# Wide attention layers: maxima and scores in two row tiles of 64, token keys in columns of their own, output projection in column tiles

## What is computed

```python
q, k, v = hidden_states @ Wq, encoder_hidden_states @ Wk, encoder_hidden_states @ Wv
logits = einsum('bhqd,bhkd->bhqk', q, k) * 64 ** -0.5
col_bias = zeros((HW, T))
col_bias = col_bias.at[:, token_indices_A].set((-20.0 * (1.0 - mask_A))[:, None])
col_bias = col_bias.at[:, token_indices_B].set((-20.0 * (1.0 - mask_B))[:, None])
probs = softmax(logits + col_bias)
out = einsum('bhqk,bhkd->bhqd', probs, v) @ Wo + bo + hidden_states
```

## Time and profile before

| | us |
|---|---|
| median of three runs | 4634.43 |
| the profiled execution: time | 4641.27 |
| the profiled execution: span, first to last instruction | 4639.5 |
| TensorE busy | 4540.8 (98%) |
| VectorE busy | 2995.0 (65%) |
| GpSimd busy | 2668.0 (58%) |
| ScalarE busy | 2266.8 (49%) |

### The profile page before, as it was taken

The page is one execution under the profiler, slowest core; times in us unless marked ns, Lnnn a source line. Parts: engine busy times, 40 slices in busy tenths (PEclk is TensorE's granted clock), DMA queues, the critical chain, the costliest instruction groups (busy, mean ns, idle before and its releaser), DMA issues.

```text
span 4639.5 us, 56326 instructions
## 1 busy us (share of the span) xinstructions
PE 4540.8 (98%) x20521; PEld 2818.1 (61%) x20521; DVE 2995.0 (65%) x5024; ACT 2266.8 (49%) x4024; POOL 2668.0 (58%) x1278
## 2 busy tenths in 40 slices
PE   8999999999999979999999999999999999999999
PEld 7888765565555445555546655555556655565554
DVE  3321477666766677777846667666757677666765
ACT  3222454454444436666655544444455544454443
POOL 0000377788778601011126887787784877788775
PEclk9999999999999979999999999999999999999999
DMA  4555832222222021111224222221216212222220
GB/s 151 177 186 163 294 74 65 63 68 54 57 63 52 12 49 26 20 26 26 60 88 135 67 52 59 63 68 41 61 45 220 62 36 67 64 68 54 57 47 28
DMA packets 121749, 356.19 MB, mean 77 GB/s; under 512 B 23925, under 2 KB 42357, under 8 KB 109690
## 3 DMA queue, kind: packets, MB, share of 16 engines
q1 hardware_dynamic: 121472, 352.59, 28.3%
HBM read 191.58 MB, written 120.31 MB: 67 GB/s over the span
## 4 chain that ended last, share of the span: by engine, by line
PE 94%; DVE 3%; DMA 1%; issue 1%; SPq 1%; ACT 0%; POOL 0%; DVEq 0%; ACTq 0%
PE ST L946 14%; PE SS L927 13%; PE ST L947 12%; PE OA L957 12%; PE OB L957 11%; PE ST L1079 5%; PE OA L1087 4%; PE SS L992 4%; PE SS L1065 3%; PE OB L1065 1%; PE SS L966 1%; PE ST L1010 1%; PE ST L1011 1%; PE ST L1012 1%; DVE mpart L1588 1%
## 5 line engine op out<-in xcount | busy, mean ns | idle before, releaser
L830 POOL TENSOR_TENSOR acc<-acc,P 128x1024 f32<-128x1024 f32 x912 | 2202.6, 2446 | 597.7 <-DVE acc L1515 584.5
L1266 ACT ACTIVATE P<-ST 128x512 f32<-128x512 f32 (+1 forms) x2496 | 1464.3, 597 | 1304.3 <-PE ST L947 1152.7
L1488 DVE TENSOR_REDUCE mpart<-SS 128x1 f32<-128x400 f32 (+1 forms) x3072 | 1628.5, 570 | 675.8 <-PE SS L927 600.5
L927 PE MATMUL SS<-KS,QS 68*128 68x400 f32 (+1 forms) x3072 | 1038.9, 372 | 11.8 <-DMA QS<-stq 10.2
L946 PE MATMUL ST<-QX,KX 128*128 128x512 f32 (+1 forms) x2496 | 1034.1, 414 | 2.7 <-ACT stw L1173 1.6
L947 PE MATMUL ST<-QS,KS 69*128 69x512 f32 (+1 forms) x2496 | 990.4, 397 | 0.0
L927 PEld LDWEIGHTS SS<-KS,QS 68*128 68x128 f32 x3072 | 584.9, 190 | 221.7 <-DVE mpart L1488 32.1
L946 PEld LDWEIGHTS ST<-QX,KX 128*128 128x128 f32 (+1 forms) x2496 | 464.1, 186 | 387.5 <-issue 286.6
L957 PE MATMUL OA<-P,Vp 128*64 128x512 f32 (+1 forms) x2496 | 658.7, 606 | 0.0
L957 PE MATMUL OB<-P,Vp 128*64 128x512 f32 (+1 forms) x2496 | 641.7, 593 | 0.0
L1348 ACT ACTIVATE PG<-ST 128x512 f32<-128x512 f32 (+1 forms) x832 | 428.0, 616 | 218.5 <-PE ST L1079 218.0
(11 more groups left out here) (238 smaller groups left out, 4240.3 us busy)
## 6 DMA issues: line engine op xcount, KB each, us to landing
q_parts<-stq SPq DMA_DIRECT2D x96, 512.0 KB, 5.1
QX<-q_parts SPq DMA_DIRECT2D x96, 512.0 KB, 11.3
KX<-k_parts SPq DMA_DIRECT2D x48, 801.0 KB, 9.2
QS<-q_parts SPq DMA_DIRECT2D x45, 512.0 KB
R<-R SPq DMA_DIRECT2D x360, 64.0 KB, 2.0
v_tiles<-sv SPq DMA_DIRECT2D x24, 832.0 KB, 6.5
Vp<-v_tiles SPq DMA_DIRECT2D x24, 832.0 KB, 7.3
k_parts<-skh SPq DMA_DIRECT2D x48, 400.5 KB, 4.9
```

Source lines behind the costliest of these rows:

```text
L830: gp.tensor_tensor(out, out, P[0:k, slot(H, t), q, :], ALU.add).then_inc(pool_a, 1)
L927: pe.matmul(SS[at % 3][:, 0:w], QS[H % 3][0:SROWS, qt * 128:(qt + 1) * 128], KS[H % 3][0:SROWS, o:o + w], start=True, stop=True).then_inc( ...
L1266: act.activation(P[0:k, slot(H, t), j, :], ST[n % 3][0:k, :], ACT.Exp, scale=SCALE).then_inc(act_p, 1)
L1488: dve.tensor_reduce(mpart[H % 2][:, i // len(KCH), c:c + 1], SS[RING_AT["s", H, i] % 3][:, 0:w], AX.X, ALU.max).then_inc(dve_ss, 1)
```

## The change

- The head dimension is 64, so the array is used as two row tiles: rows 0 to 63 (tile A) for query parts 0 and 2, rows 64 to 127 (tile B) for parts 1 and 3. Keys stand twice in SBUF (`KH` high parts, `KL` low parts, in both halves), queries are laid out by halves (`QH`, `QL`).
- A unit is now four matmuls of 64 rows (`score`, i = 0 to 3): high by high, high by low, low by high, and a fourth with the bias, mask and maximum rows (`EXK`, `EXQ`). The extra rows no longer fit beside the 64. `step_scores` interleaves the second half of one unit with the first half of the next, which is in the other row tile. The wait for `act_p` and the three banks `ST` stay.
- A maximum tile is one matmul of 64 rows; two, of different halves, go behind each other. Of a step's tiles two go beside the first half of its first unit, two beside the second half of its last, the others in pairs between.
- Token keys: 12 columns (`NTOK`) are appended to the keys, copies of the keys named by the token indices (the context is now fetched by indirect DMA with computed row numbers); their old places are masked with -1e30 in the exponential pass. Only these columns need the bias, so of the maximum tiles only the fourth range adds a small matmul of 12 columns (`EXS`). The last key tile has 78 rows, the fourth range 412 columns. The table of row numbers and the mask are computed by some 30 small VectorE operations ahead of everything else.
- The output projections are two column tiles of 64, all 4 of a step behind `values`; on VectorE their additions stand behind the step's maxima and ahead of `add`.
- Tile 3 of the denominators goes from GpSimd to VectorE, in step 2, ahead of `reciprocals`.
- Row of maxima: 4 DMAs for 1. Keys and queries of a head: 8 DMAs for 7. Two memsets and some loads move.

```diff
+S_FIRST = [14, 14, 12, 12, 12]
+S_NEXT = [10, 10, 10, 10, 10]
+S_THEN = [4, 10]
...
+def s_order():
+
+    out, at = [], [0, 0]
+    for n in S_THEN + S_NEXT:
+        for half in [1, 1] + [0, 1] * ((n - 4) // 2) + [0, 0]:
+            m = at[half]
+            at[half] += 1
+            out.append(((2 * (m // 16) + half) * 4 + m // 4 % 4, m % 4))
+    return out
...
+def s_tiles(h, g):
+
+    if g >= ROW_STEP:
+        first = sum(S_THEN[:g - ROW_STEP])
+        return 2, (range(first, first + S_THEN[g - ROW_STEP]) if h + 2 < HEADS else range(0))
+    counts = S_FIRST if h == 0 else S_NEXT
+    first = (0 if h == 0 else sum(S_THEN)) + sum(counts[:g])
+    return 1, (range(first, first + counts[g]) if h + 1 < HEADS else range(0))
...
+def o_items(h, g):
+
+    return range(4 * g, 4 * g + 4) if h % 2 == 1 and h >= 3 and g < 2 else range(0)
...
-    return [1, 2] if h + 1 < HEADS else [1, 2] + list(range(5, KT - 2))
+    return [1, 2, 3] if h + 1 < HEADS else [1, 2, 3] + list(range(6, KT - 2))
...
-    return list(range(3, KT if h + 1 < HEADS else 5))
+    return list(range(4, KT if h + 1 < HEADS else 6))
...
             def load_head_k(H):
-                b, n = H % 3, H // 2
-                sp.dma_start(words(KS[b][0:D, :]), dK[n, H % 2, 0, :, :]).then_inc(d_s[b], 16)
-                sp.dma_start(words(KS[b][D:D + NROWS, :]), dExt[H // HEADS, :, :]).then_inc(d_s[b], 16)
-
-            def load_head_b(H):
-                sp.dma_start(words(QS[H % 3][D:SROWS, :]), dBias.rearrange("m r q -> (m r) q")).then_inc(d_s[H % 3], 16)
+                for r in range(0, 128, 64):
+                    sp.dma_start(words(KH[H % 3][r:r + D, :]), dK[H // 2, H % 2, 0, :, :]).then_inc(d_s[H % 3], 16)
 
             def load_head_kx(H):
-                sp.dma_start(words(KX[H % 2][:, :]), dK[H // 2, H % 2, :, :, :].rearrange("r d k -> (r d) k"))\
-                    .then_inc(d_x[H % 2], 16)
+                for r in range(0, 128, 64):
+                    sp.dma_start(words(KL[H % 2][r:r + D, :]), dK[H // 2, H % 2, 1, :, :]).then_inc(d_x[H % 2], 16)
...
             def max_row(H):
                 sp.wait_ge(dve_ss, DVE_AT["m", H, 0])
-                sp.dma_start(words(QS[H % 3][MXROW:MXROW + 1, :]).rearrange("o (t p) -> o t p", p=128),
-                             words(mrow[:, :])).then_inc(d_m, 16)
+                for j in range(JQ):
+                    r, q = 64 * (j % 2) + MXROW, slice(j // 2 * 512, j // 2 * 512 + 512)
+                    sp.dma_start(words(EXQ[H % 2][r:r + 1, q]).rearrange("o (t p) -> o t p", p=128),
+                                 words(mrow[4 * j:4 * j + 4, :])).then_inc(d_m, 16)
...
+            gp.wait_ge(dve_tab, 22)
+            for t in range(KT):
+                gp.indirect_dma_start(c_land[0:rows_of(t), t, :], None, a["ctx"][:, :],
+                                      bass.IndirectOffsetOnAxis(ap=t_row[0:rows_of(t), t:t + 1], axis=0))\
+                    .then_inc(d_cin[t], 16)
...
             def s_tile(H, i):
-                at = RING_AT["s", H, i]
+                at, (qt, c) = RING_AT["s", H, i], s_place(H % HEADS, i)
                 if i == 0:
                     pe.wait_ge(d_s[H % 3], s_loaded(H))
+                    pe.wait_ge(d_ex, 64 * (H // HEADS + 1))
+                    pe.wait_ge(d_eq, 96)
                 wait_ring(pe, at)
-                qt, (o, w) = i // len(KCH), KCH[i % len(KCH)]
-                pe.matmul(SS[at % 3][:, 0:w], QS[H % 3][0:SROWS, qt * 128:(qt + 1) * 128], KS[H % 3][0:SROWS, o:o + w],
-                          start=True, stop=True).then_inc(pe_s, 1)
+                r, q = slice(qt // 4 % 2 * 64, qt // 4 % 2 * 64 + 64), qt // 8 * 512 + qt % 4 * 128
+                o, w = KCH[c]
+                last = pe.matmul(SS[at % 3][:, 0:w], QH[H % 3][r, q:q + 128], KH[H % 3][r, o:o + w],
+                                 start=True, stop=o + w < KP)
+                if o + w == KP:
+                    last = pe.matmul(SS[at % 3][:, w - NTOK:w], EXQ[H % 2][r, q:q + 128], EXS[r, :], start=False, stop=True)
+                last.then_inc(pe_s, 1)
...
-            def scores(H, t, j):
+            def score(H, t, j, i):
+
                 n, k = HU * H + JQ * t + j, rows_of(t)
-                if t == 0 and j == 0:
-                    pe.wait_ge(d_x[H % 2], 48 * (H // 2 + 1))
-                    pe.wait_ge(d_m, 16 * (H + 1))
-                u = n % (HU * HEADS)
-                if u < 3:
-                    pe.wait_ge(act_qw, QITEMS * (H // HEADS) + max(i for i in range(QITEMS) if i % 3 == n % 3) + 1)
-                wait(pe, act_p, n - 2)
-                bank, q = ST[n % 3][0:k, :], slice(j * 512, (j + 1) * 512)
-                pe.matmul(bank, KX[H % 2][:, t * 128:t * 128 + k], QX[H % 2][:, q], start=True, stop=False)
-                pe.matmul(bank, KS[H % 3][0:MXROW + 1, t * 128:t * 128 + k], QS[H % 3][0:MXROW + 1, q],
-                          start=False, stop=True).then_inc(pe_st, 1)
+                if i == 0:
+                    if t == 0 and j == 0:
+                        pe.wait_ge(d_x[H % 2], 64 * (H // 2 + 1))
+                    if n % (HU * HEADS) < 3:
+                        pe.wait_ge(act_qw, QITEMS * (H // HEADS) + max(i for i in range(QITEMS) if i % 3 == n % 3) + 1)
+                    wait(pe, act_p, n - 2)
+                if i == 3 and t == 0 and j == 0:
+                    pe.wait_ge(d_m, 64 * (H + 1))
+                r, q = slice(j % 2 * 64, j % 2 * 64 + 64), slice(j // 2 * 512, j // 2 * 512 + 512)
+                left, right = ((KH[H % 3], QH[H % 3]), (KH[H % 3], QL[H % 2]), (KL[H % 2], QH[H % 3]), (EXK, EXQ[H % 2]))[i]
+                last = pe.matmul(ST[n % 3][0:k, :], left[r, t * 128:t * 128 + k], right[r, q], start=i == 0, stop=i == 3)
+                if i == 3:
+                    last.then_inc(pe_st, 1)
+
+            def step_scores(H, todo, HS, tiles):
+
+                pairs, spots = (len(tiles) - 4) // 2, len(todo) - 1
+                for u in range(0, len(todo), 2):
+                    for i in range(2):
+                        score(H + todo[u][0], *todo[u][1:], i)
+                        if u > 0:
+                            score(H + todo[u - 1][0], *todo[u - 1][1:], 2 + i)
+                        elif tiles:
+                            s_tile(HS, tiles[i])
+                    for p in part(pairs, u - 1, spots) if tiles and u > 0 else range(0):
+                        s_tile(HS, tiles[2 + 2 * p])
+                        s_tile(HS, tiles[3 + 2 * p])
+                    for i in range(2):
+                        score(H + todo[u][0], *todo[u][1:], 2 + i)
+                        score(H + todo[u + 1][0], *todo[u + 1][1:], i)
+                    for p in part(pairs, u, spots) if tiles else range(0):
+                        s_tile(HS, tiles[2 + 2 * p])
+                        s_tile(HS, tiles[3 + 2 * p])
+                for i in range(2):
+                    if tiles:
+                        s_tile(HS, tiles[len(tiles) - 2 + i])
+                    score(H + todo[-1][0], *todo[-1][1:], 2 + i)
...
-                pe.matmul(SS[at % 3][:, :], wo[n % 2][:, ct * 128:(ct + 1) * 128], On[:, j * 512:(j + 1) * 512],
-                          start=True, stop=True).then_inc(pe_o, 1)
+                for c in range(0, 128, 64):
+                    last = pe.matmul(SS[at % 3][c:c + 64, :], wo[n % 2][:, ct * 128 + c:ct * 128 + c + 64],
+                                     On[:, j * 512:(j + 1) * 512], start=True, stop=True)
+                last.then_inc(pe_o, 1)
...
             def head(l, h):
                 H = l * HEADS + h
                 for g in range(STEPS):
-                    for u, (on, t, j) in enumerate(units(h, g)):
-                        scores(H + on, t, j)
-                        if takes_row(h, g, u):
-                            transpose_max(H + 1)
-                        if o_item(h, g, u) is not None:
-                            output(l * PAIRS + (h - 3) // 2, o_item(h, g, u))
-                        ahead, tiles = s_tiles(h, g, u)
-                        for i in tiles:
-                            s_tile(H + ahead, i)
+                    if takes_row(h, g, 0):
+                        transpose_max(H + 1)
+                    ahead, tiles = s_tiles(h, g)
+                    if units(h, g):
+                        step_scores(H, units(h, g), H + ahead, tiles)
                     pe.wait_ge(act_p, HU * H + JQ * (PV[g][-1] + 1))
                     for t in PV[g]:
                         values(H, t)
+                    for i in o_items(h, g):
+                        output(l * PAIRS + (h - 3) // 2, i)
                     if h + 1 == HEADS and g + 1 == STEPS:
                         last_sums(H)
...
             def head(l, h):
                 H = l * HEADS + h
                 for g in range(STEPS):
-                    for u in range(len(units(h, g))):
-                        if takes_row(h, g, u):
-                            max_row(H + 1)
```

(12 more changed lines are left out.)

337 lines of the change are left out of this document (236 added, 101 removed).

## The result

The changed kernel takes 4987.3 us (median of 4 runs, 4977.89 to 4988.98) against 4634.39 for the kernel before on the same chip: 353 us more, ratio 1.0755 (95% interval 1.0740 to 1.0769). The prediction was 4834, range 4560 to 4910: the direction is right, the size is not, +353 for +200.

What follows compares the result with a forecast made beforehand. TensorE, 94% of the span, was taken to bound the kernel. Terms 43 + 30 + 8 + 5 + 61 + 33 + 12 + 8 = +200 us on the profiled 4641.3 gave 4841, 4834 as median; range 4560 to 4910.

Steps and rivals of the forecast that it cites:

- Slot of a pair, 0.235: In the score units, matmuls in the two row tiles run together, so a pair takes 0.235 us.
- Bank loop of the scores: In score sections, matmul, exponential and next matmul in the same bank take 1.27 us, and interleaved units wait for it.
- the recurrence of a steady section: Worked-out starts in a section of eight units and ten maximum tiles: end at 5.75 us against 5.68 before, +0.07.
- VectorE, step 2 to 3: Tile 3's addition ahead of the reciprocals delays step 3's maxima: +1.45 us in 42 heads, +61 us.
- Projections: Output projections lose their stall, -8 us; their additions make VectorE late in step 1, +41; net +33 us.
- GpSimd, priced at 0, bounds to +1 a head: GpSimd's additions start a step later, but 49 us of work in 62 hides that; `sums` would wait otherwise.
- Query phases: Maximum tiles between full-array matmuls need mode changes, and ten more DMAs precede the first tile: together +12 us.
- Opening: Before the context is fetched, VectorE operations and indirect DMAs come first: +8 us, from +3 to +25.
- A: Rival: VectorE catches up and only the bank loop of the scores costs time; 4735 us, 15%.
- B: Rival: the scores' bank loop does not bind, being 0.83 us or less; 4492, or 4540 with VectorE's lateness half paid; 20%.
- C: Rival: row tiles do not run together, so units cost 2 more slots each; about 5900 us, 4%.
- D: Rival: the gains and losses cancel; 4625 to 4645 us, 6%.

Runs made afterwards that it cites:

- e5: Changed kernel with pairs of maximum tiles one group earlier, tile 3 back on GpSimd, and tile 1's and 2's additions ahead of the output additions: 4721.6 us.
- e10: e1 with each exponential of the wide layers split into two instructions of 256 columns: 4918.0 us.
- b10: Kernel before with each exponential of the wide layers split into two instructions of 256 columns: 4640.7 us.
- e1: Changed kernel with the pairs of maximum tiles one place earlier, behind groups 2, 4 and 6: 4870.8 us.
- e4: Changed kernel without the 12-column matmuls of the maxima and without the tokens' bias: 4974.7 us.
- b3: Kernel before with tile 3 of the denominators added by VectorE in step 2, ahead of the reciprocals: 4795.2 us.

## Why the prediction was wrong in size

e5 splits the sum in two. It keeps the row tiles, their order of units, the small matmuls and the projections behind `values`, moves the pairs of maximum tiles one group earlier, and takes away what VectorE adds. The terms of the prediction that it still holds are 43 + 30 + 8 + 5 - 8 + 12 + 8 = 98; e5 is 87.5 above the kernel before. The terms that it takes away are 61 + 41 = 102; the changed kernel is 265.7 above e5. **So the loop side was about right and the VectorE side, its maxima and their banks included, was 164 too small.** That 98 and 87.5 lie so close is in part luck. Between the profiled executions of e5 and of the kernel before, the heads grew by 57 for 78 (sections with tiles 28 for 43, those without 29 for 30, step 5 14 for 13, the stall of the projections -12 for -8), the query phases by 22 for 12 and the opening by 3 for 8.

Step by step:

- *Slot of a pair, 0.235*: right.
- *Bank loop of the scores*: right. Unit 3 at 1.97, sections without tiles 5.55 for 5.6, and e10 with b10 shows it as a cause. In e5 a section with tiles is 5.90, against 5.79: +0.11 for +0.17. But there the pairs stand one group earlier, and for that order e1's expectation, worked out in the same way, had 5.75: the method is right to 0.15 a section. What the small matmuls have of it is open (e4).
- *The step that failed*: the recurrence of a steady section. It followed the units from bank to bank, but let the maximum tiles go where they stood, as if a bank `SS` were always free: "pair; group 8 at 5.30; end 5.75". Three banks for tiles are counted further down in the prediction, for step 3, and nowhere else. The changed order puts four of ten tiles into the last 0.9 us, the loop of matmul, maximum and next matmul is 1.0 long, and 0.59 is the price. e1 shows 117 us of it, by an edit of nothing but places; more shows only where VectorE is on time.
- *VectorE, step 2 to 3*: mechanism right. VectorE's first maximum at 2.83, the section at 7.47 for 7.41. Against a section of 5.90 that is 1.57, for 1.45.
- *Projections*: the stall goes as said (3.87 to 3.53 for four). The lateness behind the additions is there but smaller: 1.19 in step 1 and 0.34 in step 2, 18 heads, 27 for 41 (half of the 0.34 is not theirs: step 2 is 6.65 in even heads too).
- *GpSimd, priced at 0, bounds to +1 a head*: wrong. The reason given was that 49 us of work fit into 62. They do, but when they end is set by when tile 2 (or 3) is added, and they then run beside tile 1's addition in step 1 of even heads: 1.3 in 21 heads here (28 us), some 3.6 in b3. The prediction looked for `sums` to wait; what waits is a maximum, behind an addition that takes 5.87 for 2.35.
- *Query phases*: 29 for 12. From the first to the last projection they take 84.7, 63.6 and 63.1 for 68.8, 56.9 and 56.9. In the first, more than half of the 16 is clock. Stretches before, and then after:

```profile
530.40:560.00 29.60, 29.60 (x138) 25.89 (x138) 28.89 (x56) 14.97 (x28) 16.73 (x13) 1.00 0.94 309
```

```profile
530.00:545.00 15.00, 15.00 (x39) 7.82 (x37) 7.42 (x14) 3.26 (x6) 3.81 (x3) 0.50 0.85 314
545.00:560.00 15.00, 15.00 (x51) 8.19 (x51) 9.20 (x18) 5.43 (x10) 5.10 (x4) 0.72 0.58 177
560.00:580.00 20.00, 20.00 (x88) 11.01 (x87) 16.54 (x32) 8.24 (x16) 10.24 (x8) 1.00 0.96 290
```

  Both kernels stand idle at about 520 for the first head's data and continue at 0.50. Before, the clock is back at 530.6; after, at 553, and until then three projections and two tiles take 2.2 us instead of 1.28: ten such groups, 9 us. It is no fixed price of the change: the other kernels with this query phase stood at 0.50 for 10 to 34 us and took 75.4 to 84.7 (the kernel before and its variants 7 to 10 us, 66.0 to 68.8). What sets the moment was not tried.
- *Opening*: 3.8 for 8 (the first key projection at 37.01, was at 33.21):

```profile
37.01 0.67 PE L1007 MATMUL SS<-ch,wkh 128*128 128x402 f32 x1 [1.93 <-DVE cl L1621]
```

The heads of the wide layers account for 315 of the 347 us between the two spans, the query phases for 29 and the opening for 4; 1 came back elsewhere.

Of the rivals, A (the loop alone, 4735; its own terms give 4732) is near what e5 measures, 4722. But e5 is another kernel, with three orders changed: in the changed kernel itself VectorE does not catch up, and A failed. B failed at its condition: it needed a loop of 0.83, and the trace has the 1.27 of the earlier trace rows. C failed at the pairs of starts, D with B.

No version with all of the computation beats the kernel before; the best, e5, is 1.9% slower. Its sections with tiles are 5.9 for 5.79 and those of the last head 5.55 for 4.15, and e10 shows that both kinds follow the exponential. A fourth bank for the scores, which would give the loop room, was not tried; the kernel's eight banks are three `ST`, three `SS`, `OA` and `OB`, so it would have to come from one of the others.

## What to carry to other kernels

When two streams are interleaved so that TensorE needs fewer slots, follow every ring of banks through the new order, each with its own loop (matmul, reader, next matmul) and its own number of banks: a unit that is spread over two groups holds its bank longer, and a burst of tiles at the end of a section needs as many banks as it has tiles. An engine that is 50% busy can still be late; ask what its start waits for and what its last instructions run beside. And test edits to an order together as well as one by one: here three of them gave 117, 74 and 0 alone and 266 together. Before a small difference is put down to an edit, look whether it stands where the edit is: most of e4's did not.
